# Reordering TensorE's part of a layer tile: five 512-column products in a row, Wo's product behind the turned keys

## The chip, the cores and the metric

One core of a Trainium2 chip runs the whole program. The metric is device time in microseconds (us) from launch to end, lower is better. The engines are TensorE (PE in the rows, with its weight loads as PEld), VectorE (DVE), ScalarE (ACT), GpSimd (POOL) and SyncE (SP), which here only issues DMAs. Each engine has its own instruction list and works it off in that order; they meet only in semaphores.

## The reference

The input is 16 sequences of 256 tokens of width 128. It passes a causal attention, a routed feed-forward block and a gated scan, each with a residual and a layernorm, and then six layers of local attention and feed-forward. The six layers take about two thirds of the time, and the change touches them alone:

```python
for i in range(DEPTH):                       # DEPTH = 6
    x = attn_layer(shift_tokens(x), Wqkv[i], q_scale[i], k_scale[i], Wo[i]) + x
    x = ffn_layer(shift_tokens(x), ln_g[i], ln_b[i], W1[i], b1[i], W2[i], b2[i]) + x
# attn_layer: q, k, v = split(x @ Wqkv): 16 heads of 64
#   q, k: unit length, times a scale, rotated;  softmax(8 q k^T) over windows of 32 + 32 keys;  @ v;  @ Wo
# ffn_layer: xn = layernorm(x) * g + b;  a, gate = split(xn @ W1 + b1);  (a * gelu(gate)) @ W2 + b2
```

## The kernel before

`local_attention_layers` cuts the six layers into 192 tiles of 128 tokens (6 layers, 16 sequences, 2 halves). Its software pipeline is written out by hand: every engine has a function `slot(tile)` that is run once for every tile number n, and `tile(b)` in it is tile n-b, b slots behind. So one slot of TensorE holds the first products of tile n, the scores of tile n-1, the attention of tile n-2, and so on to the last product of the feed-forward of tile n-7. The loops (`run_flat`, `run_by_layer`) hold two slots per turn. The order of the calls in `slot` is the order on the engine; nothing is scheduled by a planner.

What TensorE does in one slot, with the names used below:

- `queries`, `keys`, `values` with j = 0 or 1 (q0, q1, k0, k1, v0, v1): a product of the tile's input with a 512-column part of Wqkv, in three matmuls (L2312).
- `down` (L2520) is the last product of the feed-forward; `centred` (L2471) subtracts the mean ahead of the layernorm; `normalised_turned` (L2478) transposes the normalised tile.
- `queries_turned` and `keys_turned` (L2356, `d_rc`): 8 transposes each, called "the Q turn" and "the K turn" below; `attention_turned` and `probabilities_turned` are the same on `d_On` and `d_P`.
- `project` (L2459): Wo's product, 8 matmuls of the program that the profile counts as 16.
- `hidden_up`, `hidden_gate` (L2482), `scores` (L2391, L2398), `attend` (L2431).

PSUM has eight banks in four pairs, and nearly every call writes a bank that another engine has just read. Four waits matter here:

```python
wait(pe, "rq1_ready", t, 1)       # in values, j = 1: VectorE has rotated q1 of tile n (same bank as v1)
wait(pe, "sq0_ready", t, 1)       # in keys_turned: ScalarE has squared q0 of tile n (same pair of banks)
wait(act, "mean_done", t)         # in squares_centred: TensorE's centred product is there
wait(dve, "proj_done", t)         # in add_attention: Wo's product is there
```

ScalarE's slot goes: gelu, v0's copy, squares of q1, exponentials, `squares_centred`, a table load, `deviation` (the standard deviation), squares of k1, v1's copy, squares of q0, squares of k0, `normalised`, then the copies of the turned queries, keys, attention and probabilities. VectorE's slot goes: `add_attention` (XM), k1 rotated, the two sums of squares, `gated`, the denominators, the row maxima (`d_mx`), the inverse lengths, the centred scores, the normalised attention, q1 rotated, `add_feed_forward` (X), q0 rotated, `layernorm`, k0 rotated.

Of the kernel before, what the change touches and what calls it, by code (L numbers as in the profile page):

```python
# [2021 lines left out]
def local_attention_layers(nc, dram, X, XM, W_whole, s_w):  # L2022
# [10 lines left out]
    with ExitStack() as ctx:  # L2033
# [71 lines left out]
        def wait(eng, name, t, ahead=0, per=1, part=None):  # L2105

            tile = t.k + ahead
            if isinstance(tile, int) and not 0 <= tile < TILES:
                return
            eng.wait_ge(s[name], tile * per + (per if part is None else part) + (X_READY_AHEAD if name == "x_ready" else 0))  # L2110
# [190 lines left out]
        def _(pe):  # L2301
# [3 lines left out]
            def product(t, target, what):  # L2305

                c = CHUNK_OF[what]
                if t.first:
                    pe.wait_ge(s["w_split"], W_CHUNKS * t.l + c + 1)
                wait(pe, "xs_split", t)  # L2310
                for n, (x_part, w_part) in enumerate(((xs_high, W_high), (xs_high, W_low), (xs_low, W_high))):
                    mm = nc.tensor.matmul(target, x_part[:, t.par, :], w_part[:, c, :], start=n == 0, stop=n == 2)  # L2312
                mm.then_inc(s[f"{what}_done"], 1)

            def queries(t, j):
                if not t.live:
                    return
                if j == 1:
                    wait(pe, "g_ready", t, -6, HCH)
                    if t.edge:  # L2320
                        wait(pe, "kt_ready", t, -2)
                        wait(pe, "v1_ready", t, -2)
                        wait(pe, "rq1_ready", t, -1)
                else:
                    wait(pe, "v0_ready", t, -1)
                product(t, q_pair[:, j, :], f"q{j}")

            def keys(t, j):
                if not t.live:
                    return  # L2330
                if j == 0:
                    wait(pe, "h_ready", t, -7, HCH)
                    if t.edge:
                        wait(pe, "sk0_ready", t, -1)
                else:
                    wait(pe, "rk1_ready", t, -1)
                product(t, k_pair[:, j, :], f"k{j}")

            def values(t, j):
                if not t.live:  # L2340
                    return
                if j == 0:
                    wait(pe, "kt_ready", t, -1)
                    if t.edge:
                        wait(pe, "sq0_ready", t)
                else:
                    wait(pe, "rq1_ready", t, 1)
                    if t.edge:
                        wait(pe, "g_ready", t, -5, HCH)
                        wait(pe, "kt_ready", t, -1)  # L2350
                product(t, v_pair[:, j, :], f"v{j}")

            def turn(ps, source, done):

                for hp in range(HP):
                    mm = nc.tensor.transpose(ps[:, hp // 4, (hp % 4) * 128:(hp % 4) * 128 + 128], source(hp), ident[:])  # L2356
                mm.then_inc(s[done], 1)

            def queries_turned(t):
                if not t.live:  # L2360
                    return
                wait(pe, "finq_ready", t)
                wait(pe, "on_ready", t, -2)
                if t.edge:
                    wait(pe, "qt_ready", t, -1)
                turn(qt_pair, lambda hp: rc[:, t.par, 0, hp * 128:hp * 128 + 128], "tq_done")

            def keys_turned(t):
                if not t.live:
                    return  # L2370
                wait(pe, "fink_ready", t)
                wait(pe, "sq0_ready", t, 1)
                wait(pe, "v1_ready", t)
                if t.edge:
                    wait(pe, "v0_ready", t)
                    wait(pe, "kt_ready", t, -1)
                turn(kt_pair, lambda hp: rc[:, t.par, 1, hp * 128:hp * 128 + 128], "tk_done")
# [27 lines left out]
            def probabilities_turned(t):  # L2405
                if not t.live:
                    return
                wait(pe, "p_ready", t)
                wait(pe, "qt_ready", t, 1)
                if t.edge:  # L2410
                    wait(pe, "on_ready", t, -1)
                turn(pt_pair, lambda hp: P[:, hp, :, :].rearrange("p a d -> p (a d)"), "pt_done")
# [24 lines left out]
            def attention_turned(t):  # L2437
                if not t.live:
                    return
                wait(pe, "on_ready", t)  # L2440
                wait(pe, "xm_ready", t, -1)
                wait(pe, "xn_ready", t, -2)
                if t.edge:
                    wait(pe, "sc_ready", t, 1)
                    wait(pe, "ot_ready", t, -1)
                turn(ot_pair, lambda hp: On[:, hp, :, :].rearrange("p a d -> p (a d)"), "ot_done")

            def project(t):
                if not t.live:
                    return  # L2450
                if t.first:
                    pe.wait_ge(s["wo_in"], 16 * t.l + 16)
                wait(pe, "ot_ready", t)
                wait(pe, "x_ready", t, -3)
                if t.edge:
                    wait(pe, "sc_ready", t, 2)
                    wait(pe, "xm_ready", t, -1)
                for hp in range(HP):
                    mm = nc.tensor.matmul(proj_bank[:, 0:128], Wo[:, hp, :], OT[:, hp, :], start=hp == 0, stop=hp == HP - 1)  # L2459
                mm.then_inc(s["proj_done"], 1)  # L2460

            def centred(t):

                if not t.live:
                    return
                wait(pe, "xs2_ready", t, per=2)
                wait(pe, "sc_ready", t, 3)
                if t.edge:
                    wait(pe, "ot_ready", t, 1)
                    wait(pe, "xh_ready", t, -1)  # L2470
                nc.tensor.matmul(centred_bank[:, 0:128], xs2[:], centre[:], start=True, stop=True).then_inc(s["mean_done"], 1)  # L2471

            def normalised_turned(t):

                if not t.live:
                    return
                wait(pe, "xh_ready", t)
                nc.tensor.transpose(centred_bank[:, 128:256], xh[:], ident[:]).then_inc(s["xht_done"], 1)  # L2478
# [7 lines left out]
            def hidden_up(t):  # L2486
                if not t.live:
                    return
                if t.first:
                    pe.wait_ge(s["w1a_in"], 16 * t.l + 16)  # L2490
                wait(pe, "xn_ready", t)
                wait(pe, "sk0_ready", t, 6)
                if t.edge:
                    wait(pe, "h_ready", t, -1, HCH)
                hidden(t, W1a, up_bank, "upa_done")
# [12 lines left out]
            def down(t):  # L2508
                if not t.live:
                    return  # L2510
                if t.first:
                    pe.wait_ge(s["w2_in"], 16 * t.l + 16)
                wait(pe, "h_ready", t, 0, HCH)
                wait(pe, "sc_ready", t, 5)
                if t.edge:
                    wait(pe, "ot_ready", t, 3)
                    wait(pe, "xm_ready", t, 2)
                    wait(pe, "x_ready", t, -1)
                for c in range(HCH):
                    mm = nc.tensor.matmul(down_bank[:, 0:128], W2[0:HROWS[c], c, :], H[0:HROWS[c], c, :],  # L2520
                                          start=c == 0, stop=c == HCH - 1)
                mm.then_inc(s["down_done"], 1)

            def slot(tile):
                queries(tile(0), 1)
                keys(tile(0), 0)
                down(tile(7))
                centred(tile(5))
                queries(tile(0), 0)
                keys(tile(0), 1)  # L2530
                values(tile(1), 1)
                project(tile(4))
                normalised_turned(tile(5))
                queries_turned(tile(1))
                keys_turned(tile(1))
                hidden_up(tile(6))
                attention_turned(tile(3))
                probabilities_turned(tile(2))
                values(tile(0), 0)
                hidden_gate(tile(5))  # L2540
                scores(tile(1))
                attend(tile(2))
# [508 lines left out]
```

## Time and profile before

| | |
|---|---|
| median of 3 runs | 4449.61 us (4449.38 to 4452.7) |
| the profiled execution's own time | 4443.98 us |
| its span, first to last instruction | 4442.1 us |
| busy share of the span: PE, DVE, ACT, POOL | 90%, 79%, 75%, 62% |
| row maxima (`d_mx`), one per tile | 192, the first at 1326.2 us, the last at 4369.5 us |

The shares are means over stages of different kinds; the six layers run from about 1300 us to 4390 us. There every slot looks like the next, so the stage is read as a period: how long from one row maximum to the next, and which chain of instructions and waits makes it so long.

### The profile page before, as it was taken

The numbers are of one execution on the slowest core, as the hardware profiler recorded it, in microseconds if no ns is written. First come the engines' busy times: TensorE is split into PE (matmuls) and PEld (weight loads), VectorE is DVE, ScalarE is ACT, GpSimd is POOL, SyncE is SP. The second block draws the span as 40 slices with busy tenths as digits, with TensorE's granted clock in tenths as the row PEclk, the third lists the DMA queues.
The fourth block names the chain that finished last, engine by engine and source line by source line (L and its number), as shares of the span: only waits on it lengthen the run. The fifth ranks groups of instructions, "written<-read, shape, count | busy, mean of one in ns | idle before, by whom it ended". The sixth has DMA issues, their size and how long they took to land. (4 is left out here: it accounts for less than half of the span.)

```text
span 4442.1 us, 193023 instructions
## 1 busy us (share of the span) xinstructions
PE 3986.2 (90%) x73429; PEld 3321.3 (75%) x73441; DVE 3494.2 (79%) x6491; ACT 3339.0 (75%) x6195; POOL 2757.8 (62%) x3194
## 2 busy tenths in 40 slices
PE   7999778854678999999999999999999999999997
PEld 4555437632447888888888888888888888888886
DVE  6888373333367899999999999999999999989994
ACT  4777344432237899899988999899998999899995
POOL 3333245532236777677777777677776777677772
PEclk9999888877779999999999999999999999999999
DMA  4000135412212111211112111221112111121111
GB/s 163 1 0 0 58 116 181 140 29 96 68 41 55 43 48 49 59 51 45 50 41 70 45 46 48 58 55 46 45 49 65 48 45 46 49 66 45 46 45 40
DMA packets 141380, 254.22 MB, mean 57 GB/s; under 512 B 33985, under 2 KB 56641, under 8 KB 136641
## 3 DMA queue, kind: packets, MB, share of 16 engines
q1 hardware_dynamic: 133088, 235.11, 18.4%
q0 software_dynamic: 8192, 17.84, 1.3%
q8 instruction: 56, 0.92, 0.1%
q14 instruction: 44, 0.35, 0.0%
HBM read 70.38 MB, written 44.04 MB: 26 GB/s over the span
## 5 line engine op out<-in xcount | busy, mean ns | idle before, releaser
L2742 POOL TENSOR_TENSOR d_rc<-d_rc,d_rs 128x512 f32<-128x512 f32 x768 | 967.8, 1281 | 313.6 <-DVE d_rs L2825 276.5
L2752 POOL TENSOR_TENSOR d_rc<-d_rc,d_inv 128x1024 f32<-128x1024 f32 x384 | 723.1, 1903 | 125.9 <-DVE d_inv L2846 125.8
L2559 ACT ACTIVATE d_sq<-d_pair 128x512 f32<-128x512 f32 x768 | 454.8, 592 | 237.2 <-DVE d_rs L2825 141.0
L2312 PE MATMUL d_pair<-d_W_high,d_xs_high 128*128 128x512 f32 x1152 | 523.7, 455 | 93.1 <-issue 40.6
L2825 DVE TENSOR_TENSOR d_rc<-d_pair,d_rot 128x512 f32<-128x512 f32 x768 | 525.2, 684 | 15.8 <-ACT d_sq L2559 9.4
L2825 DVE TENSOR_TENSOR d_rs<-d_pair,d_rot 128x512 f32<-128x512 f32 x768 | 523.2, 681 | 0.0
L2312 PE MATMUL d_pair<-d_W_low,d_xs_high 128*128 128x512 f32 x1152 | 462.7, 402 | 0.9 <-issue 0.9
L2312 PE MATMUL d_pair<-d_W_high,d_xs_low 128*128 128x512 f32 x1152 | 462.2, 401 | 0.0
L2835 DVE TENSOR_REDUCE d_ss<-d_sq 128x16 f32<-128x1024 f32 x384 | 448.4, 1209 | 0.0
L2853 DVE TENSOR_REDUCE d_mx<-d_pair 128x16 f32<-128x1024 f32 x192 | 234.8, 1223 | 215.8 <-PE d_pair L2398 215.8
L2459 PEld LDWEIGHTS d_pair<-d_OT,d_Wo 128*128 128x128 f32 x3072 | 372.7, 192 | 18.4 <-issue 1.5
L2459 PE MATMUL d_pair<-d_OT,d_Wo 128*128 128x128 f32 x3072 | 374.4, 275 | 0.9 <-issue 0.8
L2356 PE MATMUL d_pair<-d_ident,d_rc 128*128 128x128 f32 x3072 | 367.3, 273 | 1.0 <-ACT d_sq L2559 1.0
L2312 PEld LDWEIGHTS d_pair<-d_W_high,d_xs_high 128*128 128x128 f32 x1152 | 221.8, 193 | 184.4 <-issue 151.4
L2356 PEld LDWEIGHTS d_pair<-d_ident,d_rc 128*128 128x128 f32 x3072 | 341.6, 141 | 2.1 <-issue 1.7
L2431 PE MATMUL d_pair<-d_VW,d_PT 64*32 64x64 f32 x18432 | 282.1, 225 | 15.8 <-issue 15.8
L2398 PEld LDWEIGHTS d_pair<-d_KT,d_QT 64*32 64x32 f32 x24576 | 254.1, 105 | 51.2 <-issue 51.2
L2398 PE MATMUL d_pair<-d_KT,d_QT 64*32 64x64 f32 x24576 | 285.8, 225 | 7.1 <-issue 7.1
L2431 PE MATMUL d_pair<-d_V,d_PT 64*32 64x64 f32 x6144 | 283.7, 226 | 2.4 <-issue 2.4
L2431 PEld LDWEIGHTS d_pair<-d_VW,d_PT 64*32 64x32 f32 x18432 | 255.1, 105 | 20.9 <-issue 12.9
L2622 ACT ACTIVATE d_OT<-d_pair 128x1024 f32<-128x1024 f32 x192 | 197.4, 1028 | 84.5 <-PE d_pair L2356 84.5
L2312 PEld LDWEIGHTS d_pair<-d_W_high,d_xs_low 128*128 128x128 f32 x1152 | 220.8, 192 | 53.3
(404 smaller groups left out, 10383.3 us busy)
## 6 DMA issues: line engine op xcount, KB each, us to landing
d_VW<-d_V SPq DMA_DIRECT2D x768, 128.0 KB, 2.4
d_VW<-d_V SPq DMA_DIRECT2D x576, 64.0 KB, 2.0
leaf_rows<-a_zeros SPq DMA_DIRECT2D x12, 1152.0 KB, 14.6
q_xrow<-leaf_rows SPq DMA_DIRECT2D x24, 576.0 KB
leaf_out<-q_yrow SPq DMA_DIRECT2D x24, 512.0 KB
d_W_whole<-Wqkv_dram SPq DMA_DIRECT2D x7, 1536.0 KB, 6.2
f_xrow<-leaf_rows SPq DMA_DIRECT2D x8, 576.0 KB, 4.0
b_table<-q_w_dram SPq DMA_DIRECT2D x4, 1024.0 KB, 7.9
```

What stands on the lines that cost most here:

```text
L2312: mm = nc.tensor.matmul(target, x_part[:, t.par, :], w_part[:, c, :], start=n == 0, stop=n == 2)
L2356: mm = nc.tensor.transpose(ps[:, hp // 4, (hp % 4) * 128:(hp % 4) * 128 + 128], source(hp), ident[:])
L2398: mm = nc.tensor.matmul(s_pair[WIN * w:WIN * w + WIN, odd, hp * DH:hp * DH + DH], QT[rows, hp, WIN * w:WIN * w + WIN], KT[rows, hp, at + W ...
L2431: mm = nc.tensor.matmul(o_pair[WIN * w:WIN * w + WIN, odd, hp * DH:hp * DH + DH], PT[rows, hp, WIN * w:WIN * w + WIN], window_values(t, w, ...
L2459: mm = nc.tensor.matmul(proj_bank[:, 0:128], Wo[:, hp, :], OT[:, hp, :], start=hp == 0, stop=hp == HP - 1)
L2559: nc.scalar.activation(sq[:, half, 512 * j:512 * j + 512], ps[:, j, :], ACT.Square).then_inc(s[f"s{qk}{j}_ready"], 1)
L2622: nc.scalar.activation(OT[:].rearrange("p h t -> p (h t)"), flat_pair(ot_pair), ACT.Copy).then_inc(s["ot_ready"], 1)
L2742: nc.gpsimd.tensor_tensor(own[:, :, a, :], own[:, :, a, :], other[:, :, 1 - a, :], ALU.add).then_inc(s[f"add{qk}_ready"], 1)
L2752: nc.gpsimd.tensor_tensor(heads(rc[:, t.par, half, :]), heads(rc[:, t.par, half, :]), inv[:, t.par, half, :].unsqueeze(2).to_broadcast([12 ...
L2825: ins = nc.vector.tensor_tensor(heads(target), heads(ps[:, j, :]), rot[:, t.par, half, cs, :].unsqueeze(1).to_broadcast([128, HP, DH]), AL ...
L2835: nc.vector.tensor_reduce(ss[:, half, :], heads(sq[:, half, :]), AX_X, ALU.add).then_inc(s[f"ss{qk}_ready"], 1)
L2853: nc.vector.tensor_reduce(mx[:], s_pair[:].rearrange("p a (h n) -> p (a h) n", n=DH), AX_X, ALU.max)\
```

## The change

Only the order of the calls in TensorE's slot changes. The operations, their sizes and their waits stay, and the other engines' lists are the same in both programs.

```diff
             def slot(tile):
                 queries(tile(0), 1)
                 keys(tile(0), 0)
-                down(tile(7))
-                centred(tile(5))
                 queries(tile(0), 0)
                 keys(tile(0), 1)
                 values(tile(1), 1)
+                down(tile(7))
+                centred(tile(5))
+                queries_turned(tile(1))
+                keys_turned(tile(1))
                 project(tile(4))
                 normalised_turned(tile(5))
-                queries_turned(tile(1))
-                keys_turned(tile(1))
                 hidden_up(tile(6))
```

TensorE's list in the loop over the tiles, before, from the third matmul of k0 on (`W_high,d_xs_low` ends a product; `H,d_W` is `down`, `centre,d_xs` is `centred`):

```order
L2312 MATMUL d_pair<-d_W_high,d_xs_low 128x512
L2520 MATMUL d_pair<-d_H,d_W 128x128 x3
L2471 MATMUL d_pair<-d_centre,d_xs 128x128
L2312 MATMUL d_pair<-d_W_high,d_xs_high 128x512
...
L2459 MATMUL d_pair<-d_OT,d_Wo 128x128 x8
L2478 MATMUL d_pair<-d_ident,d_xh 128x128
L2356 MATMUL d_pair<-d_ident,d_rc 128x128 x16
L2482 MATMUL d_pair<-d_xn,d_W1a 128x128 x2
```

The same place of the changed program, from the third matmul of v1 on:

```order
L2312 MATMUL d_pair<-d_W_high,d_xs_low 128x512
L2520 MATMUL d_pair<-d_H,d_W 128x128 x3
L2471 MATMUL d_pair<-d_centre,d_xs 128x128
L2356 MATMUL d_pair<-d_ident,d_rc 128x128 x16
L2459 MATMUL d_pair<-d_OT,d_Wo 128x128 x8
L2478 MATMUL d_pair<-d_ident,d_xh 128x128
L2482 MATMUL d_pair<-d_xn,d_W1a 128x128 x2
```

`down` and `centred` have gone behind q0, k1 and v1 (nine matmuls of 512 columns), and the sixteen transposes of the two turns stand ahead of Wo's product instead of behind it.

ScalarE's list in the same loop, in both programs, from the exponentials to the last but one of the copies (`d_sq` is a square, `d_xsq` is `squares_centred`, `d_std` is `deviation`, `d_V` is v1's copy):

```order
L2599 ACTIVATE d_P<-d_sc 128x8x64 x2
L2629 ACTIVATE d_xsq,d_xsq_sum<-d_pair 128x128
L2634 ACT_TABLE_LOAD
L2634 ACTIVATE d_preload<-d_eps 128x1
L2641 ACTIVATE d_std<-d_xsq_sum,d_eps 128x1
L2559 ACTIVATE d_sq<-d_pair 128x512
L2608 ACTIVATE d_V<-d_pair 128x512
L2559 ACTIVATE d_sq<-d_pair 128x512 x2
L2651 ACTIVATE d_xn<-d_pair,d_vecs_n 128x128
L2575 ACTIVATE d_QT<-d_pair 128x1024
L2583 ACTIVATE d_KT<-d_pair 128x8x128
```

Nothing moved here. The first of the two `d_sq` in one row is q0's, on which the K turn waits.

## Rows read from the trace of the kernel before

**Rows 1.** The page, busy time and instructions of each engine over the span.
```profile
PE 3986.2 (90%) x73429; PEld 3321.3 (75%) x73441; DVE 3494.2 (79%) x6491; ACT 3339.0 (75%) x6195; POOL 2757.8 (62%) x3194
```

**Rows 2.** Instructions on `d_mx` from 1850 to 2300 us, and VectorE's idle time before them.
```profile
L2853 DVE TENSOR_REDUCE d_mx<-d_pair x29: 1224/1225/1225, 1852.9 to 2287.5; 128x16 f32<-128x1024 f32 x29
...
  PE d_pair L2398: 31.8, 29
```

**Rows 3.** Timeline of TensorE over one slot; columns: start us, length us, instruction.
```profile
3011.70 0.49 PE L2312 MATMUL d_pair<-d_W_high,d_xs_high 128*128 128x512 f32 x1
...
3013.22 0.91 PE L2520 MATMUL d_pair<-d_H,d_W 128*128 128x128 f32 x6
3013.97 0.39 PE L2471 MATMUL d_pair<-d_centre,d_xs 128*128 128x128 f32 x2
3014.11 0.48 PE L2312 MATMUL d_pair<-d_W_high,d_xs_high 128*128 128x512 f32 x1
...
3015.64 0.47 PE L2312 MATMUL d_pair<-d_W_high,d_xs_high 128*128 128x512 f32 x1
...
3016.42 1.83 PE L2459 MATMUL d_pair<-d_OT,d_Wo 128*128 128x128 f32 x15
...
3018.20 0.27 PE L2478 MATMUL d_pair<-d_ident,d_xh 128*128 128x128 f32 x1
...
3020.05 0.83 PE L2482 MATMUL d_pair<-d_xn,d_W1a 128*128 128x128 f32 x6
...
3022.39 0.48 PE L2312 MATMUL d_pair<-d_W_high,d_xs_high 128*128 128x512 f32 x1
...
3023.93 0.39 PE L2391 MATMUL d_pair<-d_mask,d_mask_rows 64*128 64x512 bf16 x2
```

**Rows 4.** Timeline of VectorE over the same slot.
```profile
3010.30 1.23 DVE L2853 TENSOR_REDUCE d_mx<-d_pair 128x16 f32<-128x1024 f32 x1 [1.16 <-PE d_pair L2398]
...
3014.72 0.68 DVE L2825 TENSOR_TENSOR d_rs<-d_pair,d_rot 128x512 f32<-128x512 f32 x1
...
3018.69 0.29 DVE L2888 TENSOR_TENSOR XM<-X,d_pair 128x128 f32 x1 [0.18 <-issue]
...
3024.47 0.25 DVE L2872 RECIPROCAL d_rden<-d_den 128x16 f32<-128x16 f32 x1
3025.76 1.22 DVE L2853 TENSOR_REDUCE d_mx<-d_pair 128x16 f32<-128x1024 f32 x1 [1.05 <-PE d_pair L2398]
```

**Rows 5.** Timeline of ScalarE over the same slot.
```profile
3014.39 0.28 ACT L2629 ACTIVATE d_xsq<-d_pair 128x128 f32<-128x128 f32 x1
...
3017.32 0.59 ACT L2559 ACTIVATE d_sq<-d_pair 128x512 f32<-128x512 f32 x1
...
3019.12 0.45 ACT L2651 ACTIVATE d_xn<-d_pair,d_vecs_n 128x128 f32<-128x128 f32 x1
...
3020.36 1.03 ACT L2583 ACTIVATE d_KT<-d_pair 128x1024 f32<-128x1024 f32 x1
```

**Rows 6.** Timelines of three engines while the pipeline fills, 1348 to 1404 us.
```profile
1348.14 0.59 ACT L2559 ACTIVATE d_sq<-d_pair 128x512 f32<-128x512 f32 x1
...
1348.83 1.07 PE L2356 MATMUL d_pair<-d_ident,d_rc 128*128 128x128 f32 x8 [0.35 <-ACT d_sq L2559]
...
1401.68 1.95 PE L2459 MATMUL d_pair<-d_OT,d_Wo 128*128 128x128 f32 x16
...
1403.66 0.29 DVE L2888 TENSOR_TENSOR XM<-X,d_pair 128x128 f32<-128x128 f32 x1 [0.24 <-PE d_pair L2459]
```

**Rows 7.** Timeline of TensorE in the routed feed-forward block.
```profile
707.65 1.09 PE L1063 MATMUL q_ps_x<-ident,q_xrow 128*128 128x128 f32 x4 [2.28 <-ACT q_ohT L1175]
```

**Rows 8.** Stretches: busy time of each engine, then granted TensorE clock, DMA share, GB/s.
```profile
707.30:717.40 10.10, 9.75 (x47) 7.89 (x48) 4.01 (x16) 4.49 (x9) 5.66 (x6) 0.50 0.43 138
...
1828.70:1831.10 2.40, 0.08 (x2) 0.04 (x1) 2.40 (x6) 0.74 (x2) 0.78 (x2) 1.00 0.52 145
...
1396.90:1400.10 3.20, 3.20 (x10) 2.58 (x9) 2.02 (x3) 2.56 (x7) 1.53 (x1) 0.50 0.02 5
```

## The prediction

> **What bounds the kernel now.** I read the page first: over the whole span TensorE is busy 90%, and no other engine is near [rows 1]. That alone would say that TensorE's work is the bound and that an order which packs it better can gain. But the change touches only the six layers, so the second view is the period of that stage: 29 row maxima lie between 1852.9 and 2287.5 us, 434.6 us over 28 steps, 15.52 us per slot [rows 2]. In each of them VectorE stands about 1.1 us until the scores are there (31.8 us over 29) [rows 2]. The reader is to see that VectorE, the second busiest, has only this one wait per slot.
>
> The third view is the timeline of one slot. TensorE goes through it without a marked gap: q1 at 3011.70, `down` at 3013.22, `centred` at 3013.97, q0 at 3014.11, v1 at 3015.64, Wo at 3016.42, and so on to the scores' mask matmuls at 3023.93 [rows 3]. One chain ties it to VectorE. The row maximum starts at 3010.30, and VectorE then works without a stop until the second half of the rotation of q1 ends, 3014.72 + 0.68 = 3015.40: 5.10 us [rows 4]. v1 writes the bank that this rotation reads. It starts at 3015.64, 0.24 us behind it [rows 3, 4]. From v1 to the next row maximum at 3025.76 TensorE needs 10.12 us [rows 3, 4]. 5.10 + 0.24 + 10.12 = 15.46: the chain row maximum, rotation of q1, v1, Wo, turns, scores, row maximum is as long as the period. So two things bind at once: TensorE's work, and this loop through v1. What stands between v1 and the scores is on the loop, and what stands ahead of v1 (`down` and `centred` among it) is not.
>
> **What the change does to the loop, step by step.** I count from the start of v1, call it 0.
>
> 1. *Into the loop.* `down` takes 3013.22 to 3013.97, 0.75 us, and `centred` to 3014.11, 0.14 us [rows 3]. They were ahead of v1, where they filled the time until VectorE was ready. Now q0, k1 and v1 move up by 0.89 us, but v1 cannot: it still waits for q1's rotation, so TensorE stands about 1 us, and then does the 0.89 us behind v1. v1 itself is 3015.64 to 3016.42, 0.78 us [rows 3], `down` ends its issue at 0.78 + 0.75, and `centred` starts at 1.53.
>
> 2. *ScalarE comes late.* `squares_centred` waits for `centred`. It started at 3014.39 for a `centred` at 3013.97, 0.42 us later [rows 3, 5]; now at 1.95. Behind it ScalarE's list holds the table load, `deviation`, squares of k1, v1's copy and squares of q0. That chain runs without a gap from 3014.39 to 3017.32 + 0.59 = 3017.91, 3.52 us [rows 5], so q0 is squared at 5.47.
>
> 3. *The K turn waits for it.* It needs the pair of banks in which q0 lies. Before, Wo's product stood in front and the K turn came well after 3017.91. Now the Q turn starts at 1.53 + 0.14 = 1.67 and ends after half of 3018.31 to 3020.05 (3018.20 + 0.11 to 3020.05), 0.87 us, at 2.54 [rows 3]. The K turn starts 0.1 to 0.14 us behind the square: in the filling pipeline, where it already waited on ScalarE once, the square ended at 1348.73 and it started at 1348.83 [rows 6]. That gives 5.6, so TensorE stands from 2.5 to 5.6, 3.1 us in every slot. Everything else in its list is queued behind it.
>
> 4. *Wo is late, and so is VectorE.* The K turn ends at 6.5. Where VectorE waited for Wo's product, XM started 1403.66 - 1401.68 = 1.98 us after Wo's start [rows 6], so XM is at 8.46; in the present slot it came 2.27 us after Wo [rows 3, 4]. From XM to the next row maximum VectorE needs 3018.69 to 3024.47 and 0.25 more, 6.03 us at most (it waits at no other place there) [rows 4]: 14.49. TensorE's own way is as long: Wo 3016.42 to 3018.20, 1.78 us, so the transpose of `normalised_turned` is at 8.3; ScalarE goes on 0.42 us later and needs 3019.12 to 3021.39, 2.27 us, until the turned keys are copied [rows 5], 11.0; v0 waits for that copy, 0.14 later; v0 and `hidden_gate` take 3022.39 to 3023.93, 1.54 us, and the mask's start to the row maximum 1.83 us [rows 3, 4]: 14.5.
>
> 5. *The new loop.* 14.49 + 5.10 + 0.24 = 19.83 us, against 15.52: 4.3 us per slot more. POOL has no part in it: its unit lengths follow the inverse lengths, which move with the row maximum. The DMAs of the values have the whole longer slot. What the packing gives back (the first matmul of a product takes 0.32 us to the next where it follows other work, 0.23 inside a row of them; one such start fewer, 0.09 us) falls into the 1 us in which TensorE stands ahead of v1, and is worth nothing.
>
> Both v1 and `centred` are live in slots 5 to 191, 187 slots. The five layer boundaries and the ends I leave as they are. The sum against the profiled execution's 4443.98: 4444 + 187 x 4.3 = 5248 us. The median of the runs shown is 5.6 us above the profiled execution; this is far below the rest of the uncertainty.
>
> **The clock.** A 3.1 us standstill may cost more than itself. In the routed block TensorE stood 2.28 us before 707.65 [rows 7], and its clock was 0.50, the 1.2 GHz level, from 707.3 to 717.4, 1.9 us after the last matmul and for 10.1 us, though it was busy for 9.75 of them [rows 8]. While the pipeline filled a low stretch lasted 3.2 us (1396.9 to 1400.1) [rows 8]. Against it: at 1828.7 TensorE stood 2.4 us and kept 1.00, the 2.4 GHz level [rows 8]. 3.1 us is longer than either, so I take it that the clock falls in nine slots of ten. The fall comes some 1.9 us into the standstill, so 1.2 us of it cost nothing, and the rest is work at half speed, of which half is lost: (3.2 - 1.2)/2 = 1.0 us for a short stretch, (10.1 - 1.2)/2 = 4.4 for a long one, 2.7 for one in the middle. What runs then is the K turn, Wo and the transposes, all in the loop. I take the middle: 19.83 + 0.9 x 2.7 = 22.2 us per slot, 4444 + 187 x 6.7 = 5697 us. Bounds of this term: 0 gives 5248, short stretches 5430, long ones 4444 + 187 x 8.7 = 6070.
>
> The Trainium skill (TensorE: Matmul & The Clock Gate, HAM oscillation) asks for a longer standstill than 3.1 us before the clock is taken down, and by it alone the time would be the 5248 us. The trace disagrees at 707 us, with 2.28 us; so this is a rival and not the forecast.
>
> **Rivals.**
> - *Both waits bind, the clock holds* (or falls rarely): 5250 to 5350 us. For it the stretch at 1828.7, against it the one at 707.3. Chance 0.18.
> - *Only the wait ahead of v1 binds.* If squares of q0 came out early enough for the K turn, the loop grows by `down` and `centred` alone, 0.75 + 0.14: 4444 + 187 x 0.89 = 4610 us. It would need ScalarE's squares to be free of `centred`; its list puts them behind it, and the gapless chain of 3.52 us leaves no slack. Chance 0.05.
> - *Faster.* The five products in a row save the 0.09 us of a restart per slot, and nothing waits: 4444 - 17 = 4427 us. This decides if q1's rotation is finished at least 1 us earlier relative to q1's product than now, so that v1 need not wait. VectorE's 1.1 us of waiting per slot are before the row maximum, and the rotation comes after it, so I see no way for it to move up. Chance 0.03.
> - *Long low stretches*, with half of the slot at 1.2 GHz: 5900 to 6100 us. For it the four-transpose groups at 707.65, which are of the same kind as the turns and did not bring the clock back for 10 us. Chance 0.16.
>
> **How the numbers follow.** The forecast, the K turn waiting on ScalarE with the clock falling for short to middle stretches, 5350 to 5900 us, has 0.56; 0.02 is left for no change. The likeliest time is 5690. The range 5220 to 6060 takes in the sum without the clock and nearly all of the long stretches. A measurement of this kernel tells 0.2% (9 us) from no change. Slower has 0.95, the same 0.02, faster 0.03.
>
> **What would show it.** In the profile after: VectorE's row maxima 20 to 24 us apart; TensorE idle about 3 us per slot before a matmul of L2356, released by ScalarE's `d_sq`, and about 1 us before L2312, released by VectorE's `d_rs`; ScalarE idle before `d_xsq`, released by L2471; VectorE idle before XM and before X, released by L2459 and L2520, and its wait for the scores short or gone; the granted clock under 0.9 in the layers where it was 1.00. I am wrong if the idle time before L2356 is missing, that is if some other order of completion lets q0 be squared before `centred`, or if the time ahead of v1 is not lost because VectorE can run ahead.

## The result and the profile after

The changed kernel takes 5443.97 us (median of 4 runs, 5440.13 to 5450.35); the kernel before took 4449.49 us beside it. The ratio is 1.2244, 95% interval 1.2229 to 1.2259: slower by 22%. The forecast was 5690 us, within 5220 to 6060.

The page of the changed kernel, its busy line and three of its groups (line, operation, count, then busy time, mean ns, idle time of the engine before them and what ended it):

```profile
PE 4330.4 (80%) x73429; PEld 3512.0 (65%) x73441; DVE 3502.4 (64%) x6491; ACT 3338.2 (61%) x6195; POOL 2757.7 (51%) x3194
...
L2356 PE MATMUL d_pair<-d_ident,d_rc 128*128 128x128 f32 x3072 | 493.2, 314 | 523.4 <-ACT d_sq L2559 521.8
...
L2888 DVE TENSOR_TENSOR XM<-X,d_pair 128x128 f32 (+1 forms) x192 | 55.4, 288 | 725.6 <-PE d_pair L2459 725.6
...
L2459 PE MATMUL d_pair<-d_OT,d_Wo 128*128 128x128 f32 x3072 | 484.2, 325 | 0.9 <-issue 0.8
```

The work is the same as in [rows 1], instruction for instruction, and ScalarE's, VectorE's and GpSimd's busy times hardly moved. TensorE's grew from 3986 to 4330 us with no instruction more: the same matmuls took longer. And two waits have appeared that were not there: TensorE stands 522 us before the K turn, released by ScalarE's squares, and VectorE 726 us before XM, released by Wo's product.

The row maxima of the changed kernel, against [rows 2]:

```profile
L2853 DVE TENSOR_REDUCE d_mx<-d_pair x16: 1160/1160/1162, 2007.7 to 2318.0; 128x16 f32<-128x1024 f32 x16
```

310.3 us over 15 steps is 20.7 us per slot, against 15.52. The view has no idle time before them any more: the scores are there before VectorE comes.

One slot, first VectorE's timeline:

```profile
3489.46 1.16 DVE L2853 TENSOR_REDUCE d_mx<-d_pair 128x16 f32<-128x1024 f32 x1
...
3493.81 0.68 DVE L2825 TENSOR_TENSOR d_rs<-d_pair,d_rot 128x512 f32<-128x512 f32 x1
3496.70 0.35 DVE L2916 SCALAR_TENSOR_TENSOR X<-d_pair,d_vecs_a,XM 128x128 f32 x1 [2.20 <-PE d_pair L2520]
...
3503.43 0.29 DVE L2888 TENSOR_TENSOR XM<-X,d_pair 128x128 f32 x1 [2.85 <-PE d_pair L2459]
...
3509.28 1.16 DVE L2853 TENSOR_REDUCE d_mx<-d_pair 128x16 f32<-128x1024 f32 x1
```

then TensorE's:

```profile
3494.78 0.47 PE L2312 MATMUL d_pair<-d_W_high,d_xs_high 128*128 128x512 f32 x1 [0.66 <-DVE d_rs L2825]
...
3495.55 0.83 PE L2520 MATMUL d_pair<-d_H,d_W 128*128 128x128 f32 x6
3496.21 0.39 PE L2471 MATMUL d_pair<-d_centre,d_xs 128*128 128x128 f32 x2
3496.44 1.04 PE L2356 MATMUL d_pair<-d_ident,d_rc 128*128 128x128 f32 x8
...
3500.26 1.06 PE L2356 MATMUL d_pair<-d_ident,d_rc 128*128 128x128 f32 x8 [2.79 <-ACT d_sq L2559]
3501.16 1.95 PE L2459 MATMUL d_pair<-d_OT,d_Wo 128*128 128x128 f32 x16
```

and ScalarE's:

```profile
3496.64 0.28 ACT L2629 ACTIVATE d_xsq<-d_pair 128x128 f32<-128x128 f32 x1 [2.93 <-PE d_pair L2471]
...
3499.57 0.59 ACT L2559 ACTIVATE d_sq<-d_pair 128x512 f32<-128x512 f32 x1
```

Read them as one chain, against [rows 3 to 5]. The rotation of q1 ends at 3494.49, v1 starts 0.29 us later, `centred` at 3496.21, `squares_centred` at 3496.64, the squares of q0 end at 3500.16, the K turn starts 0.10 us behind them, Wo at 3501.16, XM at 3503.43, the next row maximum at 3509.28. That is 19.82 us from one row maximum to the next.

The next slot of the same timeline takes 22.39 us. Its wait is the same, but its matmuls are not:

```profile
3520.04 1.94 PE L2356 MATMUL d_pair<-d_ident,d_rc 128*128 128x128 f32 x8 [2.79 <-ACT d_sq L2559]
3521.78 3.62 PE L2459 MATMUL d_pair<-d_OT,d_Wo 128*128 128x128 f32 x16
```

The K turn takes 1.94 us instead of 1.06, and Wo 3.62 instead of 1.95. The stretches of the same kernel (TensorE's granted clock is the third number from the end) say why:

```profile
3478.40:3481.70 3.30, 2.68 (x13) 2.71 (x14) 0.84 (x2) 1.12 (x3) 1.58 (x3) 0.50 0.30 79
3481.90:3519.20 37.30, 30.59 (x678) 25.73 (x676) 27.15 (x47) 26.97 (x50) 21.89 (x26) 1.00 0.12 31
3519.40:3526.00 6.60, 5.96 (x28) 5.99 (x29) 1.14 (x3) 1.44 (x4) 1.62 (x3) 0.50 0.38 99
```

The clock was at 0.50, the 1.2 GHz level, over the K turn of one slot, at full speed through the whole of the next, and at 0.50 again in the one after. In the slot behind those it fell later, when the K turn had already begun:

```profile
3542.47 1.25 PE L2356 MATMUL d_pair<-d_ident,d_rc 128*128 128x128 f32 x8 [2.79 <-ACT d_sq L2559]
3543.51 3.43 PE L2459 MATMUL d_pair<-d_OT,d_Wo 128*128 128x128 f32 x16
```

```profile
3538.00:3543.10 5.10, 2.31 (x22) 2.10 (x21) 3.26 (x7) 3.69 (x9) 2.49 (x2) 1.00 0.00 0
3543.30:3546.50 3.20, 3.20 (x18) 3.20 (x16) 0.00 (x0) 0.20 (x1) 0.58 (x2) 0.50 0.49 126
```

Length and clock go together slot by slot. Here are five slots in a row, each from one row maximum to the next:

```profile
3489.46:3509.28 19.82, 15.89 (x360) 13.58 (x345) 14.07 (x26) 14.06 (x26) 11.87 (x15) 1.00 0.15 40
3509.28:3531.67 22.39, 18.79 (x371) 16.57 (x360) 14.15 (x25) 14.15 (x28) 11.84 (x15) 0.85 0.11 29
3531.67:3553.11 21.44, 17.63 (x370) 15.31 (x360) 14.07 (x25) 14.11 (x27) 11.85 (x15) 0.92 0.14 37
3553.11:3574.55 21.44, 17.82 (x380) 15.29 (x363) 14.16 (x26) 14.26 (x28) 11.85 (x15) 0.92 0.12 31
3574.55:3594.37 19.82, 15.91 (x360) 13.59 (x345) 14.06 (x25) 14.06 (x26) 11.83 (x15) 1.00 0.15 40
```

In VectorE's timeline the distances between the row maxima fall into three groups: of 176 regular slots 68 last 19.8 us, 86 last 21.3 us in the mean and 22 last 22.5 us; the mean of all is 20.9 us. In the trace's record of the clock every one of the 108 longer slots has a low stretch that reaches past the start of its K turn, and none of the 68 has one.

### The profile page after: what moved, and what is told of

The parts are those of the page before. It is cut to its first block and busy times, and to the rows that moved or that the text cites. A ratio compares the mean times of both kernels' runs of the same rounds, so it can differ in the third digit from the quotient of the medians.

```text
span 5438.3 us, 192931 instructions
## 1 busy us (share of the span) xinstructions
PE 4330.4 (80%) x73429; PEld 3512.0 (65%) x73441; DVE 3502.4 (64%) x6491; ACT 3338.2 (61%) x6195; POOL 2757.7 (51%) x3194
## 5 line engine op out<-in xcount | busy, mean ns | idle before, releaser
L2356 PE MATMUL d_pair<-d_ident,d_rc 128*128 128x128 f32 x3072 | 493.2, 314 | 523.4 <-ACT d_sq L2559 521.8
L2356 PEld LDWEIGHTS d_pair<-d_ident,d_rc 128*128 128x128 f32 x3072 | 409.9, 162 | 564.0 <-issue 563.4
L2888 DVE TENSOR_TENSOR XM<-X,d_pair 128x128 f32 (+1 forms) x192 | 55.4, 288 | 725.6 <-PE d_pair L2459 725.6
L2459 PE MATMUL d_pair<-d_OT,d_Wo 128*128 128x128 f32 x3072 | 484.2, 325 | 0.9 <-issue 0.8
L2459 PEld LDWEIGHTS d_pair<-d_OT,d_Wo 128*128 128x128 f32 x3072 | 477.7, 245 | 1.5 <-issue 1.5
L2651 ACT ACTIVATE d_xn<-d_pair,d_vecs_n 128x128 f32<-128x128 f32 x192 | 87.9, 458 | 574.7 <-PE d_pair L2478 574.7
L2629 ACT ACTIVATE d_xsq<-d_pair 128x128 f32<-128x128 f32 x192 | 53.3, 278 | 579.6 <-PE d_pair L2471 579.4
L2916 DVE SCALAR_TENSOR_TENSOR X<-d_pair,d_vecs_a,XM 128x128 f32 (+1 forms) x192 | 67.4, 351 | 402.6 <-PE d_pair L2520 402.6
```

Source lines behind the costliest of these rows:

```text
L2651: nc.scalar.activation(xn[:, t.par, :], centred_bank[:, 128:256], ACT.Identity, bias=vecs_n[:, 1:2], scale=vecs_n[:, 0:1]).then_inc(s["xn_ ...
L2916: nc.vector.scalar_tensor_tensor(columns(X, t), down_bank[:, 0:128], vecs_a[:, HCH:HCH + 1], columns(XM, t), ALU.add, ALU.add)\
```

## The experiments

The theory: a loop row maximum, rotation of q1, v1, `down` and `centred`, ScalarE's squares, K turn, Wo, XM, row maximum sets 19.8 us per slot, and the clock, which falls in or just behind the standstill before the K turn, adds the rest. Rivals: the time is lost to one of the two moves alone; TensorE's work is the bound; the longer slots have another cause than the clock. All of the experiments except the last two ran beside a kernel before of 4442 us; the last two ran on a chip on which it takes 4348 us, so they are compared by their ratios and their periods.

**Fill the standstill.** The changed kernel with more work for TensorE: the first turned queries 20 times more, to the same place, with the same result.

```diff
                 if t.edge:
                     wait(pe, "qt_ready", t, -1)
+                for n in range(20):
+                    hp = n % HP
+                    nc.tensor.transpose(qt_pair[:, hp // 4, (hp % 4) * 128:(hp % 4) * 128 + 128],
+                                        rc[:, t.par, 0, hp * 128:hp * 128 + 128], ident[:])
                 turn(qt_pair, lambda hp: rc[:, t.par, 0, hp * 128:hp * 128 + 128], "tq_done")
```

> The changed kernel, with 20 more transposes of the same queries to the same place ahead of the Q turn, about 2.2 us of extra TensorE work per tile that ends before the K turn may start. They leave the result as it is. Theory (loop of 19.83 us plus a clock that falls in the standstill): the standstill before the K turn shrinks from 2.79 us to about 0.6 us, the granted clock stays 1.00, every slot is 19.8 us, and the time falls from 5444 to about 5250 us. Rival (the slots of 21 to 22.4 us have another cause than the clock, or TensorE's work is the bound): extra work does not help, 5440 us or more, up to 5444 + 187 x 2.2 = 5855 us.

Measured: 5251.05 us, ratio 1.1822 (1.1802 to 1.1841). Timeline of TensorE in this kernel:

```profile
2481.62 2.35 PE L2368 MATMUL d_pair<-d_ident,d_rc 128*128 128x128 f32 x20
2483.80 1.04 PE L2356 MATMUL d_pair<-d_ident,d_rc 128*128 128x128 f32 x8
2485.44 1.06 PE L2356 MATMUL d_pair<-d_ident,d_rc 128*128 128x128 f32 x8 [0.60 <-ACT d_sq L2563]
```

its row maxima:

```profile
L2857 DVE TENSOR_REDUCE d_mx<-d_pair x16: 1160/1160/1160, 2018.2 to 2315.9; 128x16 f32<-128x1024 f32 x16
```

and stretches of 320 us, first of this kernel:

```profile
2000.00:2320.00 320.00, 294.59 (x5852) 255.20 (x5850) 228.11 (x387) 228.94 (x422) 192.11 (x227) 1.00 0.15 39
```

then of the changed kernel:

```profile
2000.00:2320.00 320.00, 263.35 (x5479) 226.22 (x5479) 219.45 (x374) 220.22 (x403) 182.69 (x218) 0.95 0.16 44
```

TensorE does 2.2 us more per slot, 192 times, and the kernel is 193 us faster than the changed one (187 us by the two ratios, as the kernel before took 4449 us beside the one and 4442 us beside the other). The clock is 1.00, and the slot 297.7 / 15 = 19.85 us. Against the slots of 21 to 22 us only the transposes in the gap and the clock differ: the fall costs about 190 us, and the loop alone stands at the 5250 us that its sum gave. TensorE's work as the bound is excluded.

**Wo's product behind the turns, alone.** `down` and `centred` go back to their old place.

```diff
                 keys(tile(0), 0)
+                down(tile(7))
+                centred(tile(5))
                 queries(tile(0), 0)
                 keys(tile(0), 1)
                 values(tile(1), 1)
-                down(tile(7))
-                centred(tile(5))
                 queries_turned(tile(1))
```

> Half of the change alone: Wo's product and the transpose of the normalised tile behind the Q and K turns, while down and centred stay where they were before. Theory: counted from v1, the K turn must wait for the squares of q0 until 2.4 us instead of starting at 1.65, a standstill of 0.75 us, and Wo's end moves from 2.56 to 5.0 us, so that XM comes at 5.25 and the next row maximum at 11.25 instead of 10.12: 16.6 us per slot, clock at 1.00, 4444 + 187 x 1.1 = 4650 us. Rival (Wo's place is free, all of the loss comes from down and centred): 4450 us.

Measured: 4675.14 us, ratio 1.052 (1.0502 to 1.0538). Timeline of TensorE and then of VectorE:

```profile
2484.09 1.06 PE L2356 MATMUL d_pair<-d_ident,d_rc 128*128 128x128 f32 x8 [0.63 <-ACT d_sq L2559]
2484.99 1.95 PE L2459 MATMUL d_pair<-d_OT,d_Wo 128*128 128x128 f32 x16
```

```profile
2487.26 0.29 DVE L2888 TENSOR_TENSOR XM<-X,d_pair 128x128 f32 x1 [2.72 <-PE d_pair L2459]
```

The slot is 16.8 us against 16.6 expected. The wait is where it was placed, 0.63 us for 0.75. XM comes 2.27 us after Wo's start and not 1.98 as in [rows 6]; this 0.29 us is more than the whole difference, and a shorter way from XM to the row maximum (5.84 us, expected 6.0) takes a part of it back.

**The five products in a row, alone.** Wo's product and the transpose of the normalised tile go back ahead of the turns.

```diff
                 down(tile(7))
                 centred(tile(5))
-                queries_turned(tile(1))
-                keys_turned(tile(1))
                 project(tile(4))
                 normalised_turned(tile(5))
+                queries_turned(tile(1))
+                keys_turned(tile(1))
```

> The other half alone: the five products in a row, then down and centred, with Wo's product ahead of the turns as before. Theory: Wo's product and a wait for the normalised tile (until 4.7 us after v1) fill most of the time until the squares of q0 are there, so that the K turn at 5.7 us does not wait for ScalarE; TensorE stands about 1.25 us before the transpose of the normalised tile and the clock holds; next row maximum at 12.3 us, 17.65 us per slot, 4844 us. So the two halves together cost more than their sum (about 200 and 400 against 995 us). Rival (the halves add up, and this one carries what the other does not): 4444 + 995 - 206 = 5240 us.

Measured: 4871.93 us, ratio 1.0969 (1.095 to 1.0987). Its row maxima, and what TensorE waited for in a slot:

```profile
L2853 DVE TENSOR_REDUCE d_mx<-d_pair x18: 1225/1225/1225, 2012.3 to 2314.3; 128x16 f32<-128x1024 f32 x18
```

```profile
2230.88 0.47 PE L2312 MATMUL d_pair<-d_W_high,d_xs_high 128*128 128x512 f32 x1 [0.90 <-DVE d_rs L2825]
2233.06 2.05 PE L2459 MATMUL d_pair<-d_OT,d_Wo 128*128 128x128 f32 x16 [0.36 <-DVE X L2916]
2235.45 0.33 PE L2478 MATMUL d_pair<-d_ident,d_xh 128*128 128x128 f32 x1 [0.34 <-DVE d_xh L2897]
2235.61 1.91 PE L2356 MATMUL d_pair<-d_ident,d_rc 128*128 128x128 f32 x16
```

302.0 / 17 = 17.76 us per slot, against 17.65 expected. With Wo's product in front, the K turn waits for nobody (its 8 transposes follow the Q turn's in one row of 16); the lost time lies ahead of v1, ahead of Wo (which also waits for X, a wait that I had passed over) and ahead of the transpose. The halves cost 233 and 429 us, together 662; the whole change costs 995. Of the 333 us between them about 190 are the clock. The other 140 fit that only both moves together leave TensorE nothing to do while ScalarE squares: the wait before the K turn is 0.63 us with the one, none with the other and 2.79 us with both.

**ScalarE's squares first.** The changed kernel with another order on ScalarE.

```diff
                 squares_centred(tile(6))
-                load_sqrt(tile(6))
-                deviation(tile(6))
                 squares(tile(1), 1, "k", 1)
                 take_values(tile(2), 1)
                 squares(tile(1), 0, "q", 0)
+                load_sqrt(tile(6))
+                deviation(tile(6))
```

> The changed kernel, with ScalarE's list reordered: squares of k1, v1's copy and squares of q0 ahead of the table load and the standard deviation instead of behind them. Theory: the K turn starts at 4.2 us after v1 instead of 5.35 (the squares then wait for VectorE's rotation of q0), the standstill is 1.7 us, too short for most of the clock's falls, but the standard deviation comes 1.8 us later and VectorE reaches XM at 7.6 and the row maximum at 13.6 us: 18.95 us per slot, 5085 us. Rival (the K turn waits for something else than this chain): no change, 5440 us.

Measured: 5210.62 us, ratio 1.173 (1.171 to 1.175). Timeline of TensorE:

```profile
2213.86 1.06 PE L2356 MATMUL d_pair<-d_ident,d_rc 128*128 128x128 f32 x8 [1.58 <-ACT d_sq L2559]
...
2218.19 0.90 PE L2482 MATMUL d_pair<-d_xn,d_W1a 128*128 128x128 f32 x6 [1.37 <-ACT d_sq L2559]
```

The K turn's wait shrank to 1.58 us, as expected, so it is ScalarE's chain that it waits for. The time is 126 us over the expectation, and the second row says where it went: `hidden_up` waits 1.37 us for the squares of k0. They need k0 rotated, which VectorE does behind the layernorm, and the layernorm is what this order makes late. The slot is 19.66 us on average and not 18.95. I had followed the delay to XM and not to this wait.

**`down` and `centred` ahead of v1.** The kernel before, with these two calls moved behind q0 and k1 only.

```diff
                 keys(tile(0), 0)
-                down(tile(7))
-                centred(tile(5))
                 queries(tile(0), 0)
                 keys(tile(0), 1)
+                down(tile(7))
+                centred(tile(5))
                 values(tile(1), 1)
```

> The kernel before, with down and centred moved behind q0 and k1 but left ahead of v1: four products in a row, and nothing more between v1 and the scores than before. Theory (what costs is work put between v1 and the row maximum, and the late squares of centred on ScalarE): the first part is absent; centred is 1.5 us later, so that the squares of q0 end 3.8 us after v1 and the K turn loses about 0.4 us; VectorE reaches the layernorm 1.3 us later, and the transpose of the normalised tile stands about 0.5 us. Row maxima 15.9 to 16.1 us apart, about 4442 + 187 x 0.5 = 4535 us; the clock holds. Rival (any place of down and centred behind k1 costs as much as in the five-product kernel): 4870 us. Second rival (the time was lost to v1's wait alone): 4442 us.

Measured: 4451.82 us, ratio 1.0233 (1.0219 to 1.0248); the expectation, 4535 us beside 4442, is a ratio of 1.021. Its row maxima:

```profile
L2853 DVE TENSOR_REDUCE d_mx<-d_pair x13: 1223/1224/1225, 2290.4 to 2483.4; 128x16 f32<-128x1024 f32 x13
```

193.0 / 12 = 16.08 us per slot, within the 15.9 to 16.1 expected. The sum was met, but not term by term, as TensorE's timeline shows:

```profile
2314.80 0.33 PE L2478 MATMUL d_pair<-d_ident,d_xh 128*128 128x128 f32 x1 [0.28 <-DVE d_xh L2897]
2314.97 1.91 PE L2356 MATMUL d_pair<-d_ident,d_rc 128*128 128x128 f32 x16
```

The transpose of the normalised tile waits, 0.28 us in this slot and not the 0.5 expected. The K turn, which was to lose 0.4 us, waits for nothing: both turns run in one row of 1.91 us, as before. Over 16 slots TensorE takes about 0.3 us longer than before from Wo's product to that transpose, and about 0.2 us longer from `centred` to v1, which the expectation did not name. That the sum came out right is in part luck. So with the two calls on one side of v1 the cost is 2.3%, with them on the other side (the five products in a row, 17.76 us) 9.7%. One call in the list decides, the one that waits for VectorE.

**Half of the filling.** As the first experiment, with `range(10)`.

> As the kernel that fills the standstill, with 10 extra transposes instead of 20, 1.1 us instead of 2.2 us, so that TensorE stands about 1.7 us before the K turn. Theory: shorter than every standstill after which the clock fell in the traces so far (2.28 us and more), and as long as the one in the kernel with ScalarE's squares first, where it held (1.58 us): the clock holds, 19.85 us per slot and 5250 us as with 20. Rival (the clock wants most of the gap filled): between 5251 and 5444 us, with row maxima 21 us apart in part of the slots.

Measured: 5155.16 us, ratio 1.1852 (1.1831 to 1.1873), beside 1.1822 (1.1802 to 1.1841) with 20. Stretch, wait before the K turn, and row maxima:

```profile
2000.00:2320.00 320.00, 277.17 (x5701) 238.31 (x5702) 226.02 (x385) 227.17 (x418) 190.43 (x227) 1.00 0.14 37
```

```profile
2218.56 1.06 PE L2356 MATMUL d_pair<-d_ident,d_rc 128*128 128x128 f32 x8 [1.70 <-ACT d_sq L2563]
```

```profile
L2857 DVE TENSOR_REDUCE d_mx<-d_pair x16: 1160/1160/1164, 2009.3 to 2307.0; 128x16 f32<-128x1024 f32 x16
```

Within the stage a standstill of 1.70 us per slot leaves the clock at 1.00 and the slot at 19.85 us; one of 2.79 us does not. The two fillings are the same within the stage. Their ratios differ by 0.003 because the kernel before has less time outside the layers on this chip, so the same loss weighs more (the first row maximum is at 1237.7 us in the one with 10 and at 1321.8 in the one with 20).

The length of the standstill alone does not decide, though. The expectation's "2.28 us and more" overlooked the third stretch of [rows 8], which came behind a standstill of 2.06 us, and in the kernel with 20 transposes, where a new layer begins, the clock fell behind one of 1.59 us:

```profile
1940.53 0.67 PE L2312 MATMUL d_pair<-d_W_high,d_xs_high 128*128 128x512 f32 x1 [1.59 <-DVE d_rs L2829]
```

```profile
1940.70:1943.90 3.20, 3.20 (x13) 2.91 (x13) 0.53 (x2) 0.11 (x1) 0.00 (x0) 0.50 0.00 0
```

## Why the prediction was right, and where it was off

**What bounds the kernel now.** Right as far as it was tried. The loop through v1 was taken as equal to the period, and every experiment that put work between v1 and the row maximum lengthened the slot. That the loop already binds in the kernel before rests on the equal lengths alone: TensorE shows no idle time ahead of v1 there, and moving `down` and `centred` to just ahead of v1, off this loop, cost 0.56 us per slot as well.

**Step 1, the wait ahead of v1.** Right in place, about 1 us forecast, 0.66 and 0.79 us in the two slots looked at, and 0.29 us and not 0.24 from rotation to v1.

**Steps 2 and 3, ScalarE late and the K turn waiting.** Right: 5.6 us after v1 forecast, 5.48 measured; a standstill of 3.1 forecast, 2.79 as the profile counts it. The experiment with the squares first shows that it is this chain, and the two halves show that it takes both moves.

**Steps 4 and 5, the new loop.** 19.83 us forecast, 19.82 measured, but two of its terms cancel: from Wo's start to XM it is 2.27 us and not 1.98, and from XM to the row maximum 5.85 and not 6.03, while the K turn came 0.1 earlier. The sum without the clock, 5248 us, was met by the kernel with the filled standstill at 5251.

**The clock.** The mechanism was right and its size was not. This is the term of the sum that was off: the prediction took it that the clock falls in nine slots of ten and that each fall costs 2.7 us, 2.4 us per slot. It fell so that 108 of 176 slots, six of ten, were longer, by 1.7 us in the mean ((86 x 21.3 + 22 x 22.5) / 108 = 21.5, less 19.8), 1.06 us per slot. The cost of one fall came out as 1.5 us in 86 slots and 2.7 us in 22. The prediction gave 1.0 us to a short one, since 1.2 us of the low stretch were to lie in the standstill; in the slots shown it began between 3519.2 and 3519.4, 0.7 us before the K turn, and between 3543.1 and 3543.3, 0.7 us behind the K turn's start, so that nearly all of it was work. In the stretches shown the clock was low for 6.6 and 3.2 us; the 10.1 us of the routed block was not a guide for a slot that goes on with this stage's work. The 5430 us that the prediction gave for short stretches come nearest to the result by luck: falls at 1.0 us each in nearly all slots weigh as much as falls at 1.7 us in six of ten. Nor are its bounds worked out alike: 5430 and 6070 us come out with a fall in every slot, 5697 with one in nine of ten. Why it falls in some slots and not in others, with the same 2.79 us of standing in each, was not tried and stays open.

**The rivals.** That the clock holds gives 5250: it is what filling the standstill does, and not what this kernel does, whose time lies near the lower end of the 5350 to 5900 us that went with a falling clock. Long low stretches, with half of the slot at 1.2 GHz, did not come. Of the signs named, one was not met: the granted clock was to be under 0.9 in the layers, and was 0.95 over the stretch of 320 us. That only the wait ahead of v1 binds is excluded by the 522 us before the K turn. The saving of 0.09 us per slot for a restart less is there in the trace at most inside a wait. The rule of the Trainium skill (TensorE: Matmul & The Clock Gate, HAM oscillation), by which the standstill was too short to bring the clock down, disagrees with this trace: with 2.79 us it came down, in six slots of ten.

## What to carry to other kernels

In a hand-written pipeline in which several engines are nearly full, find the loop of waits that is as long as the period, and ask of each call to be moved on which side of the waiting instruction it lands; the same two calls, 0.89 us of work, cost 2.3% ahead of the instruction that waits and 9.7% behind it (with Wo's product where it was). Then follow what the moved call releases on the other engines down their lists, for the next wait is often for something that merely stands behind it, here squares behind a standard deviation. A restart saved on TensorE is worth nothing while it has to stand for VectorE anyway.

## What the runs showed of the hardware

Work that is thrown away can save time: 20 transposes more per slot, 192 times, made the changed kernel 193 us faster, since they kept TensorE's clock at its 2.4 GHz level through a wait. Ten, which left 1.70 us of standing, did it as well, on the other chip (ratio 1.185 against the 1.224 of the changed kernel). Two halves of a change can cost 233 and 429 us and the whole 995.
